# A graph layer's thin last slots: nine gathers of GpSimd become register-addressed row copies issued by SyncE

## The reference

```python
def _pna_layer(h, src, dst, Mw, Mb, Uw, Ub, bn_g, bn_b, mix_w, mix_b):
    msg = jnp.concatenate([h[src], h[dst]], axis=-1) @ Mw.T + Mb
    s1 = jax.ops.segment_sum(msg, dst, num_segments=N)
    s2 = jax.ops.segment_sum(msg * msg, dst, num_segments=N)
    mx = jax.ops.segment_max(msg, dst, num_segments=N)
    mn = jax.ops.segment_min(msg, dst, num_segments=N)
    ...  # std and var from s1, s2 and the degree
    agg = jnp.concatenate([mx, mn, std, var], axis=-1)
    h_neigh = jnp.concatenate([agg, agg * (logd / DELTA), agg * (DELTA / logd)], axis=-1)
    u = jnp.concatenate([h, h_neigh], axis=-1) @ Uw.T + Ub
    ...  # batch norm over the nodes
    return jax.nn.leaky_relu(u @ mix_w.T + mix_b, 0.01) + h
```

## Time and profile before

| | us |
|---|---|
| median of 3 runs | 2186.88 (2179.98 to 2197.56) |
| the profiled execution, its own time | 2167.94 |
| its span, first to last instruction | 2166.1 |
| setup, until the first gather of layer 0 | 135.9 |
| layer 0, first to last gather issued | 602.7 |
| layers 1 and 2, the same | 578.0 and 578.1 |
| last gather of layer 1 to the first of layer 2 | 81.3 |

### The profile page before, as it was taken

One profiled execution on the slowest core, in us unless ns is written; L12 is line 12 of the kernel. 1 busy time (PEld: TensorE's weight loads), 2 busy tenths in 40 slices (PEclk: granted clock), 3 DMA queues, 4 the chain that ended last, 5 costly groups with the idle time before them and its releaser, 6 DMA issues.

```text
span 2166.1 us, 14665 instructions
## 1 busy us (share of the span) xinstructions
PE 1219.2 (56%) x4692; PEld 874.3 (40%) x4692; DVE 710.3 (33%) x1711; ACT 313.7 (14%) x807; POOL 1286.6 (59%) x1344
## 2 busy tenths in 40 slices
PE   6520675655546683175575637485156556646585
PEld 5310453444434452153453525353145344434452
DVE  8800423333222352042232413253033223223344
ACT  0110410110000144010100100035011000000015
POOL 2756477666766406666666666604757767667604
PEclk9995788777777796587786868697578878678798
DMA  6253233333333213323233333203323333233300
GB/s 61 70 147 92 59 97 92 89 87 94 98 84 92 61 46 115 92 85 95 88 94 94 87 95 92 86 27 116 104 73 93 94 89 96 86 92 95 92 10 30
DMA packets 88488, 183.62 MB, mean 85 GB/s; under 512 B 31790, under 2 KB 47489, under 8 KB 88409
## 3 DMA queue, kind: packets, MB, share of 16 engines
q0 software_dynamic: 61264, 164.22, 26.8%
q1 hardware_dynamic: 27150, 18.51, 3.9%
HBM read 169.06 MB, written 14.98 MB: 85 GB/s over the span
## 4 chain that ended last, share of the span: by engine, by line
another core or an unknown queue 46%; PE 28%; issue 12%; ACT 7%; DVE 5%; POOL 1%; DMA 0%; SPq 0%; DVEq 0%; ACTq 0%; POOLq 0%
PE ps L689 12%; PE ps L712 7%; PE ps L699 2%; ACT base L830 1%; PE ps L709 1%; PE ps L674 1%; PE ps L754 1%; PE ps L639 1%; PE ps L719 1%; PE ps L739 1%; ACT msq L846 1%; ACT u_sb L863 1%; ACT agg L850 0%; ACT base L828 0%
## 5 line engine op out<-in xcount | busy, mean ns | idle before, releaser
L548 POOL DMA_INDIRECT G<-p_by_rank,index x812 | 796.0, 980 | 525.6 <-issue 227.4
L689 PE MATMUL ps<-G,wide_ident 128*128 128x256 f32 x2436 | 634.6, 410 | 19.8 <-DMA G<-p_by_rank,index 12.2
L689 PEld LDWEIGHTS ps<-G,wide_ident 128*128 128x128 f32 x2436 | 499.5, 209 | 122.1 <-issue 17.5
L548 POOL DMA_INDIRECT G<-p_by_node,index x406 | 399.7, 985 | 217.5 <-issue 129.3
L712 PE MATMUL ps<-w_u_sb,aggT 128*128 128x384 f32 x600 | 266.6, 598 | 217.8 <-issue 137.0
L1261 DVE SCALAR_TENSOR_TENSOR u_sb<-ps,amp,u_sb 128x128 f32<-128x128 f32 x75 | 26.3, 351 | 824.4 <-ACT u_sb L863 599.7
L712 PEld LDWEIGHTS ps<-w_u_sb,aggT 128*128 128x128 f32 x600 | 137.9, 236 | 341.8 <-issue 200.8
L699 PE MATMUL ps<-wide_ident,agg 128*128 128x128 f32 x300 | 61.3, 339 | 339.8 <-ACT agg L850 254.2
L699 PEld LDWEIGHTS ps<-wide_ident,agg 128*128 128x128 f32 x300 | 42.2, 171 | 364.3 <-ACT agg L850 268.7
L719 PE MATMUL ps<-wide_ident,u_sb 128*128 128x128 f32 x75 | 23.8, 318 | 181.9 <-DVE u_sb L1263 101.2
L1140 DVE TENSOR_TENSOR acc<-G 128x512 f32<-128x512 f32 x150 | 96.4, 684 | 39.7 <-DMA G<-p_by_rank,index 38.5
(11 more groups left out here) (202 smaller groups left out, 1158.0 us busy)
## 6 DMA issues: line engine op xcount, KB each, us to landing
G<-p_by_rank,index POOLq DMA_INDIRECT x812
G<-p_by_node,index POOLq DMA_INDIRECT x406
p_by_rank<-base SPq DMA_DIRECT2D x12, 512.0 KB, 3.0
p_by_node<-G SPq DMA_DIRECT2D x6, 514.0 KB
w_u_sb<-in_w_u SPq DMA_DIRECT2D x3, 768.0 KB
x_r<-rows_by_rank SPq DMA_DIRECT2D x1, 1600.0 KB
windows<-src_pad SPq DMA_DIRECT2D x1, 1118.0 KB, 25.1
index<-rows_by_rank SPq DMA_DIRECT2D x1, 468.0 KB
```

The costliest lines, as they stand in the source:

```text
L548: g.indirect_dma_start(G[:, n % R, j, 0:w], None, table, bass.IndirectOffsetOnAxis(ap=index[:, t, k0 + j:k0 + j + 1], axis=0))\
L689: ins = mm(out_ps, ident[:, :], G[:, n % R, k, 0:2 * D], start=False, stop=n in END and k == nk - 1)
```

## The change

Nine slots of a layer are taken from GpSimd: one each of tiles 11, 16, 18, 21, 22 and 23, and three of tile 24. They are last slots of their tiles, in which few nodes still have an arc; `held` bounds how many rows such a slot needs (mean + 2 spreads + 3), rounded up to 16, and the cheapest are taken until 720 rows are spent: 64, 112, 96, 80, 64, 96, 96, 64 and 48 rows. GpSimd's slots go from 406 to 397 a layer, its groups from 111 to 109, and the list has 118 entries with the nine.

So that the rows in use come first in a tile, the setup turns the order inside each tile around (one more multiply and one exclusive or of the ranks on VectorE).

SyncE fetches the nine in three phases of 3 slots (272, 240 and 208 rows). In each it loops over chunks of 16 rows: one load of 16 numbers into registers, then 16 DMAs, one row each, from the table of p into a DRAM buffer `stage`. After a phase's rows have landed, one DMA a slot brings them from `stage` into one of 7 places of `X` on the chip. The row numbers come from small tables, `sp_node` in layer 0 and `sp_rank` afterwards, filled by 9 DMAs each. The nine entries stand behind the first two or three groups of their tile. Space for `X` comes from the ring, which goes from 16 groups to 14.

```diff
+SP_ROWS, SP_FROM, UNIT = 720, 6, 16
...
-    R = 16
+    R, NX = 14, 7
+    WHOLE = [n for n, g in enumerate(GROUPS) if g[4] == P]
+    BYROW = [n for n, g in enumerate(GROUPS) if g[4] < P]
+    PHASES = [BYROW[i:i + 3] for i in range(0, NB, 3)]
...
+            def fetch_rows(l, i):
+                numbers, table, w = (sp_rank, p_table, 2 * D) if l else (sp_node, p0_table, W)
+                first = AT[PHASES[i][0]] // UNIT
+                many = sum(GROUPS[n][4] for n in PHASES[i]) // UNIT
+                with sp.Fori(first, first + many) as c:
+                    _, rows_of = nc.values_load_multi_w_load_instructions(
+                        bass.at_runtime_partition(numbers[0:1, :], c), engines=[mybir.EngineType.SP],
...
+                    for j, row in enumerate(rows_of):
+                        sp.dma_start(stage[bass.ds(c * UNIT + j, 1), 0:w],
+                                     table[bass.ds(row, 1), :]).then_inc(row_here[i].sem, 16)
+                sp.wait_ge(row_here[i].sem, row_here[i].at(l, row_here[i].per_layer))
+                for n in PHASES[i]:
+                    if n in LAST_USER:
+                        sp.wait_ge(dve_used.sem, dve_used.at(l, LAST_USER[n] + 1))
+                        sp.wait_ge(pe_used.sem, pe_used.at(l, LAST_USER[n] + 1))
...
+                    sp.dma_start(X[0:m, OWN[n], 0:w], stage[AT[n]:AT[n] + m, 0:w]).then_inc(by_row[OWN[n]].sem, 16)
...
-            for l in range(L - 1):
-
-                sp.wait_ge(p_added.sem, p_added.at(l, 0))
-                sp.dma_start(w_p_sb[:, :], w_p[l + 1]).then_inc(s_wc, 16)
-                sp.dma_start(b_p_sb[:, :], b_p[l + 1:l + 2, :].to_broadcast([P, D])).then_inc(s_wc, 16)
+            for l in range(L):
+                if l < L - 1:
+
+                    sp.wait_ge(p_added.sem, p_added.at(l, 0))
+                    sp.dma_start(w_p_sb[:, :], w_p[l + 1]).then_inc(s_wc, 16)
+                    sp.dma_start(b_p_sb[:, :], b_p[l + 1:l + 2, :].to_broadcast([P, D])).then_inc(s_wc, 16)
+
+                if l == 0:
+                    sp.wait_ge(s_spnode, 16 * NB)
+                    sp.wait_ge(s_pstored, 16 * NC)
+                else:
+                    sp.wait_ge(p_stored.sem, p_stored.at(l - 1, 16 * NC))
+                    if l == 1:
+                        sp.wait_ge(s_sprank, 16 * NB)
+                for i in range(len(PHASES)):
+                    fetch_rows(l, i)
+                if l == L - 1:
+                    break
+                if l == 0:
+                    for s, n in enumerate(BYROW):
+                        t, _, k0, _, m = GROUPS[n]
+                        sp.wait_ge(rank_kept.sem, rank_kept.at(0, n + 1))
+                        sp.dma_start(listed(sp_rank, n), index[0:m, t, k0:k0 + 1],
+                                     allow_slow_non_contiguous=True).then_inc(s_sprank, 16)
 
                 sp.wait_ge(z_done.sem, z_done.at(l, T))
                 update_weights(l + 1)
...
+                    got = G[:, RING[n], k, 0:2 * D] if n in RING else X[0:m, OWN[n], 0:2 * D]
+                    ins = mm(out_ps, ident[0:m, :], got, start=False, stop=n in END and k == nk - 1)
...
+                if n in OWN:
+                    dve.wait_ge(dve_used.sem, dve_used.at(l, n))
+                    row = X[0:m, OWN[n], 0:D]
+                    TT(acc[0:m, 0, 0, :], acc[0:m, 0, 0, :], row, ALU.max)
+                    TT(acc[0:m, 1, 0, :], acc[0:m, 1, 0, :], row, ALU.min).then_inc(dve_used.sem, 1)
+                    return
```

More of the change, by code:

```diff
@@ L61, in slot_plan, with held @@
         most = 0.05 if t == 0 else P * t
-        plan.append(next(k for k, b in enumerate(beyond) if b <= most))
-    return [max(k, 8) for k in plan[::-1]]
+        plan.append(max(next(k for k, b in enumerate(beyond) if b <= most), 8))
+    plan = plan[::-1]
+    def held(t, k):
+        b = beyond[k]
+        spread = math.sqrt(b * max(1.0 - b / n_nodes, 0.0))
+        return min(P, max(math.ceil(b + 2.0 * spread + 3.0) - P * (n_tiles - 1 - t), 1))
+    return plan, held
 def build(nc, x, src, dst, w_p, b_p, w_q, w_h, w_u, w_mix, v_cols, out):
@@ L81, in build @@
     assert PADS and PLAN[T - 1] > 0
+    PART, left = [[] for _ in range(T)], SP_ROWS
+    for m, t, k in sorted((held(t, k), t, k) for t in range(SP_FROM, T) for k in range(PLAN[t])):
+        m = -(-m // UNIT) * UNIT
+        if m <= left and m < P:
+            PART[t].insert(0, m)
+            left -= m
+    for t in range(T):
+        PLAN[t] -= len(PART[t])
+    HELP = min([PADS] + PART[T - 1][-1:])
     STRIDE = 8
@@ L316, in build @@
         gathered = [Signal(sem(f"gathered{i}"), slot_total[i]) for i in range(R)]
+        row_here = [Signal(sem(f"rows_staged{i}"), 16 * sum(GROUPS[n][4] for n in ns)) for i, ns in enumerate(PHASES)]
+        by_row = [Signal(sem(f"fetched_by_row{i}"), row_total[i]) for i in range(NX)]
         dve_used = Signal(sem("groups_compared"), NG)
@@ L426, in mix_weights @@
                 sp.dma_start(v_sb[:, :], of_layer(v_cols, l)).then_inc(s_wa, 16)
+            def fetch_rows(l, i):
[5 more added lines that the diff above has]
+                        bass.at_runtime_partition(numbers[0:1, :], c), engines=[mybir.EngineType.SP],
+                        min_val=0, max_val=NP - 1,
+                        skip_runtime_bounds_check_because="node numbers and ranks below NP")
+                    for j, row in enumerate(rows_of):
[7 more added lines that the diff above has]
+                        if l == 0:
+                            sp.wait_ge(rank_kept.sem, rank_kept.at(l, LAST_USER[n] + 1))
+                    m = GROUPS[n][4]
+                    sp.dma_start(X[0:m, OWN[n], 0:w], stage[AT[n]:AT[n] + m, 0:w]).then_inc(by_row[OWN[n]].sem, 16)
@@ L1034, in _ @@
             ch.wait()
-            v.tensor_copy(rank_i[:, :], small[:, 4, :])
-            v.tensor_copy(p_nat[:, :, 2 * D], small[:, 4, :]).then_inc(s_info, 1)
+            ch.step(v.tensor_copy(rank_i[:, :], small[:, 4, :]))
+            ch.wait()
+            ch.step(TS(bits_i[:, 0, :], rank_i[:, :], P, P - 1, ALU.is_ge, ALU.mult))
+            ch.wait()
+            ch.step(TT(rank_i[:, :], rank_i[:, :], bits_i[:, 0, :], ALU.bitwise_xor))
+            ch.wait()
+            v.tensor_copy(p_nat[:, :, 2 * D], rank_i[:, :]).then_inc(s_info, 1)
             def win(i, t0, t1, w, o=0):
```

136 lines of the change are left out of this document (88 added, 48 removed).

## The result

The changed kernel took 3429.82 us (median of 4 runs, 3414.59 to 3440.98) against 2188.59 us (2179.98 to 2197.56) for the kernel before: ratio 1.568, 95% interval 1.561 to 1.574. It is 1241 us slower; 2162 was forecast. The profiled execution took 3423.48 us, its span is 3421.8.

A forecast was written before the change was run, and what follows sets the result against it. GpSimd's issue of gathers was taken to set the pace, TensorE close behind. 2167.9 - 27 (nine slots) + 1 (setup) = 2142 for the profiled execution; the median, 19 higher, gives 2161, rounded to 2162 us; range 2145 to 2225.

The forecast's parts named there:

- SyncE's row sum: SyncE's loop: one row costs 0.65 us (0.36 to 0.92), from DMA, gap, register instruction and a share of the load.
- The deadlines: SyncE's 720 rows are in time up to 0.72 us a row in layer 0, 0.80 in layers 1 and 2.
- Rival 3: SyncE's rows are late, from 0.72 us a row: 2220 us, 2478 at the bound of 0.92; chance 0.20.
- the delay counts in full: If SyncE's rows are late, TensorE, VectorE, ScalarE and soon GpSimd stand, so all the lateness adds to the time.
- wrong altogether: Sign against the whole forecast: the loop's rows, through the semaphore or DRAM writes, take over 1 us each.
- Until then the cost is nothing: SyncE's loop in stage a: as long as the rows arrive in time, they cost 0.
- Rival 4: SyncE's small transfers slow the gathers or TensorE further: +51 us, 2238 us; chance 0.08.
- The ring's 0 to +9 us a layer: Gather ring cut from 16 to 14 groups: costs 0 to 9 us a layer, value taken 0.
- the nine slots' 9 us a layer: Nine gathers fewer on GpSimd gain 9 us a layer, between 6.8 and 11.3; -27 for three layers, ends 0 and -39.
- layer 0 as a sign that GpSimd leads: Layer 0's early GpSimd stop was 16.6 us longer, its gathers 24.7 longer; time never won back, so GpSimd's issue sets the pace.
- The coupling: While GpSimd issues gathers TensorE progresses slowly; when the full ring pauses GpSimd, it catches up: speed 0.39 against 0.85.
- the gathers' spacing and number: GpSimd's gathers: 397 a layer, still 1.25 us apart.

The follow-up runs named there:

- e4_side: e2_plain plus a SyncE loop of 240 register-addressed row transfers a layer that nobody reads: 2258.8 us, ratio 1.031 to the kernel before.
- e2_plain: Changed kernel without the row loop, nine slots loaded from consecutive (wrong) table rows by one transfer each: 2162.1 us, ratio 0.988 to the kernel before.
- g3_plain: The same kernel as e2_plain, run in another session: 2134.1 us against 2177.7 for the kernel before, ratio 0.983.
- e1_ring14: Kernel before with a gather ring of 14 groups in place of 16, nothing else: 2173.8 us against 2196.4, ratio 0.992.
- e6_nops: e2_plain plus a SyncE loop of 2000 turns with only counter and branch, no transfers: 2986.9 us, ratio 1.362 to the kernel before.
- e10_ahead12: Kernel before, ring still 16 places, but GpSimd waits for the group 12 back: 1888.5 us against 1888.6, ratio 1.000.

## Why the prediction was wrong, point by point

- **The failed step is SyncE's row sum.** It was 0.65 us, bounds 0.36 to 0.92. Measured without gathers: 0.95 in layer 0, already past the bound. The transfer with addresses from registers takes 0.60 by node and 0.52 by rank, not the 0.41 of a plain one. The two MOVEs, the FUSED_REGOPS and the gaps make 0.28, where 0.10 had been set for one register instruction and one gap. The load of 16 registers (median 1157 ns) is 0.07 a row, half of the 0.14 taken. And beside gathers the row is at 2.0, which no term had in it: the bounds came from single instructions, and no row showed SyncE working through a run of gathers.
- **The deadlines held.** Put 1.39 and 1.35 into the prediction's own working, 2162 + 720 x (1.39 - 0.72) + 2 x 720 x (1.35 - 0.80) = 3436; 3430 was measured. It holds layer by layer: from first gather to first gather, and from the last layer's first to the end, the changed kernel needs 474, 386 and 391 us more than before, where the working gives 473, 387 and 387 (the delay less 9). By the same working the unslowed row, 0.95 in layer 0 and 0.89 in the later ones, would have given 2162 + 166 + 130 = 2458. So of the loss over the forecast an estimated 300 us are plain length and 970 are the slowing beside gathers. Rival 3 had the mechanism and the direction, and "the delay counts in full" was right; its size stood at 58 us, and at 316 for its far end. The sentence on what would make the forecast "wrong altogether", rows over 1 us, is what came.
- **"Until then the cost is nothing" is wrong.** `e4_side` has 240 rows a layer, all in time, and pays 97 us over `e2_plain`, 0.13 us for each of the 720. By the sum above it does not come on top in the changed kernel, where TensorE waits for X anyway. Rival 4 had seen that the small traffic could hold up TensorE. That it is the traffic is not shown: fixed transfers with the same bytes pay less than half, 42 us.
- **The ring's 0 to +9 us a layer had the wrong sign; the nine slots' 9 us a layer is not settled.** `e2_plain` and `g3_plain` gain 34 and 44 us with both and the setup in it, where 26 were forecast; that `e2_plain` hit 2162 is luck, as it is 34 us off 2196 in place of 26 off 2187, and the two terms' errors cancel in part. The ring alone gives 23 (`e1_ring14`, same session as `e2_plain`). That leaves 12 us for the slots there, 4 a layer, and with the same 23 for the ring 21 in `g3_plain`, 7 a layer; the intervals of `e1_ring14` and `e2_plain` overlap, so the split is rough. I had read layer 0 as a sign that GpSimd leads. But its gathers wait for ScalarE's ranks too, 37.2 us in 18 waits (`ACT index L837`), which the other layers' do not, so that comparison did not single out GpSimd; and the ring tests say that TensorE's backlog at the last gather is part of the end as well.
- **The coupling was read rightly, and its reason went unasked.** "While gathers are issued TensorE progresses slowly" was in the text, from the earlier trace rows. Had the same been asked of SyncE, which would for the first time work beside the gathers, the row's upper bound would have been far above 1 us. The Trainium skill (SBUF — State Buffer, section "SBUF: two separate sides") that was weighed there rules out contention of compute and DMA at the memory's ports. The counter loop of `e6_nops` touches no memory and is slowed all the same, so that rule, right or not, did not bear on it. That TensorE's late results have the same cause is likely (on chip 12 both are missing, and in `e6_nops` a transpose waits 42 us for its answer while SyncE's branches take 698 ns), and not shown.
- **Right:** the gathers' spacing and number, where each layer first needs the third phase, and what queues behind a late row. The setup, forecast at +1 us, has its first gather at 141.1 against 135.9 in the two profiles.

What stays open: by what mechanism gathers slow SyncE's instructions, through their issue or their transfers, and why on some chips only; which part of a row's loop holds up TensorE; what the changed kernel would take on the chip without the slowing (the written-out form lost 10.6% there, and its rows are shorter).

## What to carry to other kernels

An idle engine's queue is not free time: before work is moved to it, measure one turn of the new loop by itself and once beside what will run with it, since both numbers exceeded every bound drawn from other rows here. Compare the gain an item brings (9 slots, some 4 to 7 us a layer) with the instructions it costs (720 rows of four and more): neither 720 nor 176 rows paid, looped or written out. And try a shorter run-ahead as well as a longer one, since what stands in the ring at the last load is still to be worked off; it gained up to 2.6% where gathers slow the rest, and nothing on chip 12.

## What was not expected of the hardware

- Beside GpSimd's indirect transfers every kind of instruction that SyncE's loops hold (MOVE, FUSED_REGOPS, ALU_OP, COMPARE_BRANCH, the DMA's issue) is lengthened now and then, up to 1678 ns for a MOVE of 29 in the stretch shown. It is little in the first 5 us after GpSimd resumes and heaviest from 15 us on, where an empty turn of 0.25 us takes 1.6 and more. Per instruction this averages some 0.2 to 0.3 us: 1.05 for the four and more of a looped row, 0.55 for the three of a written-out one, 0.64 for the two of an empty turn (in the stretches shown).
- One chip of four does not show it: the same kernel before took 1889 us there instead of 2169 to 2196. In `e10_ahead12`, its nearest relative with a trace from that chip, GpSimd waits 2.1 us in layer 1, where it waits 69 in the kernel before (62.8 for "remote", 6.2 for TensorE). A comparison between sessions is worth nothing without the kernel before in each.
- One load of 16 registers from the on-chip memory took 1.16 us in layer 0 and 0.99 in layer 1, 0.07 and 0.06 a register. The Trainium skill (Runtime: NRT & Kernel Launch, "Instruction fetch mechanics") has about 0.2 a register even in bulk, and describes these as loads from DRAM (HBM); the runs have no row for those.
